# The first batch's last state sums inside the last head group, and its chain ahead of the second batch's behind the loop

## What is computed

```python
x = x + L0_xattn(layernorm(x), ctx, ctx)      # 16 heads, 2048 keys, causal
x = x + L0_attn(layernorm(x), ...)            # state space scan, 16 states
x = x + L0_ffn(layernorm(x), ...)             # router, top 2 of 16 low rank experts
x = x + L1_xattn(layernorm(x), ctx, mask)     # one head, 2048 keys, masked
x = x + L1_attn(layernorm(x), ...)            # 16 heads, local window, compressed blocks, rotary tables
x = x + L1_ffn(layernorm(x), ...)             # top 2 of 8 experts of three layers
```

```python
x_proj = einsum('bld,ed->ble', x, W_xproj)
dt = softplus(x_proj[..., :256]); B = x_proj[..., 256:272]; C = x_proj[..., 272:]
A = -exp(A_log)
h = exp(dt * A) * h + dt * B * x              # per token, 256 channels x 16 states
y = einsum('bdn,bn->bd', h, C) + D * x
```

## Time and profile before

| | us |
|---|---|
| median of 3 runs | 481.57 (479.76 to 482.05) |
| profiled execution | 479.39 |
| its span, on which all times inside the trace are counted | 477.6 |
| PE busy | 417.9 |
| DVE busy | 331.0 |
| ACT busy | 270.2 |
| POOL busy | 103.5 |

### The profile page before, as it was taken

One profiled execution on the slowest core, in us unless ns is written; L12 is line 12 of the kernel. 1 busy time (PEld: TensorE's weight loads), 2 busy tenths in 40 slices (PEclk: granted clock), 3 DMA queues, 4 the chain that ended last, 5 costly groups with the idle time before them and its releaser, 6 DMA issues.

```text
span 477.6 us, 9148 instructions
## 1 busy us (share of the span) xinstructions
PE 417.9 (87%) x3661; PEld 308.8 (65%) x3661; DVE 331.0 (69%) x537; ACT 270.2 (57%) x596; POOL 103.5 (22%) x86
## 2 busy tenths in 40 slices
PE   0178799998979898998999999997999799999997
PEld 0125466666646586567543654347999699999996
DVE  3888775769576975987239843874775587787772
ACT  4404888775848834740233724557950566777752
POOL 3002257001078001000003320440020302333300
PEclk9999999999999999999999999999999989999999
DMA  6599185455553054707500000009400884540000
GB/s 232 128 242 298 20 221 151 124 123 145 149 207 86 1 179 132 289 2 301 228 0 0 2 1 0 0 8 355 168 1 2 279 286 149 183 160 2 1 2 22
DMA packets 25003, 58.28 MB, mean 122 GB/s; under 512 B 5210, under 2 KB 13690, under 8 KB 21115
## 3 DMA queue, kind: packets, MB, share of 16 engines
q1 hardware_dynamic: 24960, 57.69, 37.9%
HBM read 44.77 MB, written 0.29 MB: 94 GB/s over the span
## 4 chain that ended last, share of the span: by engine, by line
PE 71%; DVE 14%; ACT 8%; issue 5%; DMA 2%; SPq 0%; POOL 0%; ACTq 0%; DVEq 0%; POOLq 0%
PE ps L1300 19%; PE ps L1101 10%; PE ps L930 7%; PE ps L917 5%; PE ps L886 4%; DVE mx L1677 3%; PE ps L1009 3%; ACT reg_b L679 3%; PE ps L1256 3%; PE ps L965 2%; PE ps L1098 1%; PE ps L1027 1%; PE ps L1246 1%; PE ps L1245 1%; PE ps L1153 1%
## 5 line engine op out<-in xcount | busy, mean ns | idle before, releaser
L1677 DVE TENSOR_REDUCE mx<-ps 128x1 f32<-128x1024 f32 x64 | 77.0, 1221 | 36.6 <-PE ps L886 25.3
L679 ACT ACTIVATE reg_b<-ps 128x512 f32<-128x512 f32 x128 | 75.2, 598 | 28.2 <-PE ps L917 19.8
L917 PE MATMUL ps<-qreg,reg_b 98*128 98x128 bf16 x512 | 46.9, 225 | 5.2 <-ACT reg_b L679 3.8
L1300 PE MATMUL ps<-part_a 128*128 128x256 f32 x384 | 48.2, 283 | 0.4 <-DVE part_a L1834 0.4
L1101 PE MATMUL ps<-reg_b,xT 128*128 128x512 f32 x96 | 47.6, 618 | 0.0
L917 PEld LDWEIGHTS ps<-qreg,reg_b 98*128 98x128 bf16 x512 | 35.5, 100 | 18.5 <-ACT reg_b L679 8.9
L1300 PEld LDWEIGHTS ps<-part_a 128*128 128x128 f32 x384 | 46.9, 192 | 0.6 <-DVE part_a L1834 0.6
L828 ACT ACTIVATE reg_a<-ps,b 128x256 f32<-128x256 f32 x64 | 30.2, 471 | 26.4 <-PE ps L1300 26.4
L930 PE MATMUL ps<-reg_b 128*32 128x128 f32 x1024 | 43.2, 286 | 0.0
L886 PE MATMUL ps<-reg_b,qreg 96*128 96x512 bf16 x96 | 34.1, 424 | 10.3 <-DMA reg_b<-reg_b 7.5
L1834 DVE TENSOR_TENSOR part_a<-reg_a,part_a 128x256 fp32r<-128x256 f32 x64 | 26.9, 436 | 23.2 <-ACT part_a L831 23.2
(11 more groups left out here) (279 smaller groups left out, 857.0 us busy)
## 6 DMA issues: line engine op xcount, KB each, us to landing
reg_b<-in_w SPq DMA_DIRECT2D x16, 512.0 KB, 8.5
reg_b<-in_w SPq DMA_DIRECT2D x8, 1024.0 KB, 7.8
reg_b<-reg_b SPq DMA_DIRECT2D x56, 128.0 KB, 3.5
reg_b<-in_w_qkv SPq DMA_DIRECT2D x3, 2048.0 KB, 7.4
reg_b<-reg_a SPq DMA_DIRECT2D x40, 128.0 KB, 3.1
reg_a<-in_ctxK SPq DMA_DIRECT2D x4, 1024.0 KB, 7.0
reg_a<-in_ctx SPq DMA_DIRECT2D x8, 512.0 KB, 5.0
reg_b<-bc_mem SPq DMA_DIRECT2D x4, 1024.0 KB, 5.6
```

The source lines that it names most:

```text
L679: sc.activation(pT[n % 3], score_b[n % 2], ACT.Exp).then_inc(S("exp_done"), 1)
L917: mm = pe.matmul(cols, kS[g % 3][0:SROWS, c // 8, j, P * (c % 8):P * (c % 8 + 1)], qT[b][0:SROWS, HPG * hg + j, :], start=not last, stop=True)
L1300: mm = pe.matmul(out, left[u], right[v], start=(i, u, v) == (0, 0, 0), stop=(i, u, v) == (len(terms) - 1, 0, 1))
L1677: ve.reduce_max(mx[:, piece // 2, piece % 2:piece % 2 + 1], score_a[m % 2].rearrange("p i k -> p (i k)"), X_AXIS).then_inc(S("max_done"), 1)
```

## The change

Nothing is computed otherwise. On PE the state sums of half 0 start one pair of chunks earlier (beside chunks 7, 9, 11, 13), half of the sums of half 1 goes beside chunk 15, and the other half between the last values and `outputs_to_rows`. Behind the loop batch 0's norm, transpose and first products go ahead of batch 1's on every engine; `tables()` on DVE moves forward from behind `add_inputs(1)` to the place where `state_input(0)` stood, and `state_input(0)` goes behind `ln_apply(3, 0)`. The fillers get other counts. SP issues eleven loads of `tab_in` ahead of `bias0` and the keys of batch 0, once the last scores of the loop are made; `wkv`, `b_kv` and `b3` are counted on `lora_in`, and their users wait for that.

```diff
+            sp.wait_ge(S("score_b"), NCH * NG)
             load(cos2, io["cos2"], "tab_in")
...
             load(b_c, io["bc"].unsqueeze(0), "tab_in")
 
+            sp.wait_ge(S("hc_done"), KD)
+            load(bias0, io["bias0"].partition_broadcast(P), "ssm_in")
+            load(ctxT[:, 0, :, :], io["ctxT"][0].rearrange("(h p) k -> p h k", p=P), "ctxT_in0")
+
+            sp.wait_ge(S("x_done1"), 1)
+            load(wkv, io["wkv"].rearrange("(k p) n -> p k n", p=P), "lora_in")
...
             spread_maps(1)
...
+            inv_sqrt(2, 0)
             inv_sqrt(1, 1)
-            inv_sqrt(2, 0)
...
+            transposed_x(2, 0)
+            hidden_exp(0)
             transposed_x(1, 1)
-            transposed_x(2, 0)
             copy_z(1)
             softplus_exp(1)
-            hidden_exp(0)
+            gap_exp(0)
             softplus_log(1)
+            wxaT(0)
             exp_table()
...
             for i in range(4):
-                beside[7, 9 + 2 * i] = [(sum_states, 0, 0, range(4 * i, 4 * i + 4))]
+                beside[7, 7 + 2 * i] = [(sum_states, 0, 0, range(4 * i, 4 * i + 4))]
+            beside[7, 15] = [(sum_states, 0, 1, range(NS // 2))]
...
             values(NG - 1, NCH - 1)
+            sum_states(0, 1, range(NS // 2, NS))
             outputs_to_rows(NG - 1)
...
-            sum_states(0, 1)
-            keep_busy(7, 18)
+            keep_busy(7, 20)
+            x_to_columns(2, 0)
+            keep_busy(7, 4)
+            lora_products(0)
             x_to_columns(1, 1)
...
             def tables():
+                ve.wait_ge(S("tab_in"), 176)
...
             add_inputs(0)
+            add_states(0)
+            ln_stats(2, 0)
             weigh_outputs(1)
+            ln_apply(2, 0)
             normalise(1)
...
-            state_input(0)
+            tables()
             lora_add(0)
             ln_stats(3, 0)
             bias_parts()
             ln_apply(3, 0)
+            state_input(0)
             scan(1, 0)
+            max3(0, 0)
             state_input(1)
-            max3(0, 0)
             max3(0, 1)
```

## The result

| | before | after |
|---|---|---|
| median of 6 runs, us | 480.8 (479.69 to 482.05) | 477.03 (475.97 to 478.56) |
| profiled execution, us | 479.39 | 478.56 |
| its span | 477.6 | 476.8 |
| its mean granted clock of TensorE | 0.986 | 0.982 |

The changed kernel takes 0.9926 of the time of the one before, with a 95% interval of 0.9897 to 0.9955: 3.8 us less by the medians. The forecast was 480.5 and 1.1 us of gain, the range 477.7 to 482.4.

A forecast was written before the change was run, and what follows sets the result against it. PE bounds the kernel (71% of the chain), DVE has 14%. Gains of 0.1 and 1.0 us make 1.1: 479.39 becomes 478.3 us profiled, plus 2.2 carried to the median gives 480.5, range 477.7 to 482.4.

The forecast's parts named there:

- The loop's end: At the end of the loop, batch 0's state sums would end at 178.3 instead of 179.6, gaining 1.3 us.
- The third rival: Sums in the loop delay ACT's last exponentials, so the loop doesn't give its 1.3 us: 481.8 us, chance 0.09.
- Batch 0 up to its third norm: Behind the loop, batch 0's third norm would move from 197.75 to about 196.35, 1.4 us gained.
- What is late next: On DVE, the scan waits for ACT's decays, so the second maximum comes at 208.1 against 208.23: gain shrinks to 0.1 us.
- the first rival: DVE doesn't hold the second maximum, as with decays made sooner: 2.5 us gained, 479.1 us, chance 0.12.
- The rest: Up to batch 0's fourth-norm transpose, moving `tables()` removes PE's wait: 1.0 us more, 1.1 us in sum.
- The step that failed: Profiled forecast 478.3 us plus the 2.2 us by which the old profiled execution lay under its median: 480.5 us.
- The wait of 1.11 us goes: PE's wait for DVE's norm ahead of batch 0's transpose at 224.91 would vanish.
- The second rival: TensorE's clock falls behind a 1.3 us stand ahead of `exp3(0)`'s transposes: 0.5 us slower, 482.1 us, chance 0.18.
- the fourth rival: B's read back through memory lands late and holds up the scan by 1.45 us: 481.9 us, chance 0.05.
- The rule on the table load: On ACT, the skill's 1380 ns drain per table switch would cut the gain to 0.6 us; the trace's 1.28 us was taken.

The follow-up runs named there:

- e7: Changed kernel with `tables()` back between `add_inputs(1)` and `add3(0)`: ratio to the old kernel 0.9966, section 67.37 us.
- e2: Changed kernel run and profiled once more, nothing edited: ratio to the old kernel 0.996.
- e3: Changed kernel with the state sums back at their old places in and behind the loop, the new order behind it kept: ratio to the old kernel 0.9991.
- e11: Changed kernel with 18 fillers between the first and second layer of the first expert, in the wait at 378: ratio to the old kernel 0.9928.
- e8: Changed kernel with 13 instead of 8 of the first half's decays ahead of ACT's copy of the third transpose: ratio to the old kernel 0.9933.
- e4: Old kernel with only the state sums moved into the loop, the order behind it as before: ratio to the old kernel 1.0083.
- e6: Old kernel with 16 more fillers ahead of `lora_logits(0)` and 10 ahead of batch 0's fourth transpose: ratio to the old kernel 0.9966.
- e12: Changed kernel with 13 decays ahead of the copy, twelve more fillers ahead of the third transpose and 18 in the expert layer: ratio to the old kernel 0.9881.
- e1: Old kernel run and profiled once more, nothing edited: ratio to itself 1.0008.

## Why the prediction was right or wrong

**The loop's end** held. The sums of half 1 were to start at 173.9 and did at 174.81 - 0.88 = 173.93; they were to end at 178.3 and did at 178.37. The third rival, a loop that doesn't give its 1.3 us, fell with that.

**Batch 0 up to its third norm** held: `add_states(0)` forecast 178.4, measured 178.64; `lora_hidden(0)` 184.65 and 184.67; the third norm 196.35 and 196.49. The loads for the tables made no one wait.

**What is late next** held: scan 200.15 and 200.32, second maximum 208.1 and 208.25 without a wait, p3's transposes behind a wait of 1.3 and 1.34. Eight decays behind the copy decided it, as the first rival's condition said, and five more decays ahead of it gave 1.11 us. That rival was put at 2.5 us in all; with its condition made true the section is shorter by 68.41 - 65.99 = 2.4.

**The rest** held in its sum, 1.1 forecast and 1.31 measured in the section, but not in its reasons. The transpose was to start at 223.8 and did at 224.53 - 0.88 = 223.65. I had taken a length of 3.73 us for the state sums, while the transpose starts 3.57 us behind their start. And I gave the credit to the tables. The runs showed what that move does. In after batch 0 is no earlier at p3's transposes than before (53.65 us behind the first mark, and 211.12 - 157.49 = 53.63 by the row below) and gains at the norm behind them; with the tables back (e7) it is 1.03 earlier at the transposes and gains nothing more. The move takes the lead away in front and gives it back behind. PE before, at these transposes:

```profile
211.12 2.19 PE L1019 MATMUL ps<-cf,reg_b 128*128 128x128 f32 x16
```

**The step that failed** is the last of the sum: "I carry the difference over to the median: 480.5 us." The profiled execution itself was forecast at 478.3 us and took 478.56, in part by luck, since it came 0.88 us late into the section. The step then added 2.2 us, because before's profiled execution lay that far under the median of three runs. After's lay 478.56 - 477.03 = 1.5 us above its median of six. These 2.2 + 1.5 = 3.7 us, less the 0.3 by which the profile was missed, are the whole way from 480.5 to 477.03. Of the 2.2, 0.8 were the small sample: with six runs the median of before is 480.8, not 481.57. The rest of the two offsets goes with the clock. After's profiled execution had a mean granted clock of 0.982, its other five runs 0.986 to 0.993; before's had 0.986, where all its runs have a mean of 0.982. The bound of the range, 477.7, allowed 1.5 us for the median's own moving. The median of after's six runs lies 0.7 us under that bound, and the mean of all 18 runs, 478.3, lies in the range.

**A term that was missing** stands in "The wait of 1.11 us goes", priced at its length alone. I had read that the clock stayed at 1.00 behind it and took this for a property of the place. It was one execution. In 3 of 10 traces the clock fell there, for 1.64 us. The second rival counted a fall of the clock only for the new kernel, with the old one as if it had none; so about half a microsecond, by the estimate above, had no term. The same mistake stands in the fourth rival: the read back of B was priced as a risk of after, and was in the way of before, by 0.52 us in one of six traces. Both together would have moved the forecast by 0.6 us, which is the smaller part of the miss.

**The second rival** fell. PE waits 1.33 to 1.35 us ahead of p3's transposes in five traces (after, e2, e3, e7, e11), and the clock fell behind none of them.

**The rule on the table load.** The load at 192.80 took 1.28 us and the next ACT instruction began 1.29 us after its start, as at the earlier trace rows. No drain shows. The 1380 ns of the Trainium skill, "ScalarE: Activation LUTs", section "What ACT_TABLE_LOAD costs", are not in these traces, and the working by the row was the better one.

**What was on either side of the section** was to stay as it was. It did: from the second mark to batch 1's scores 28.92 us in both profiled executions.

## What to carry to other kernels

Follow the section between two marks that the change doesn't touch, in each trace, and put it beside the medians: here the section repeated within 0.15 us, but for one wait of 0.52 that the trace named, while whole executions moved by over 3 us. When the clock may fall behind a wait of PE, price the wait in the old kernel too, by its length and by the share of executions in which a fall follows, and look at several executions for that share. Don't carry one execution's distance from its median over to another kernel: see first where its granted clock lies among those of the other runs. And when work is put ahead of an engine's copy for the path, count what was moved behind it: five small ACT instructions behind it cost 1.1 us, nearly what the section won.

## What the runs showed of the hardware

- **A wait's length alone doesn't decide whether the clock falls.** Behind 1.11 us (and 0.55 more, a product later) it fell to 1.2 GHz in 3 of 10 traces, behind 1.34 us in none of 5, behind 1.47 us (ahead of the third transpose in after, e2, e3, e8 and e11) in none of 5, behind 1.82 us in 5 of 9, behind 2.1 us in 15 of 16, and in e11, where the filler had made 0.70 of that, once more. The same wait in the same kernel has a fall in some executions and not in others. What PE did ahead of the wait differs between these places: 26 fillers stand ahead of the wait of 1.34, state sums ahead of that of 1.11. Whether that decides was not tested.
- **Falls came in one size.** In all 18 traces a fall is 3.4 us at 0.50, which takes 1.7 us worth of full clock, or two of these in a row; only the one at the end of the span is shorter. Its price hangs on the place: 1.64 us in the projections at 228, 1.4 us at 185 in e4, 0.1 us at 188, where fillers and waits stand behind it.
- **In the last block** a fall is on the path. From the product behind the wait at 378 to the end it is 96.06 us without a fall (e2), 96.8 to 98.3 with one and 98.1 to 98.8 with two.
- **Products that nobody reads can win time.** With nothing but 26 of them more in two waits of before (e6) the ratio was 0.9966 (0.9937 to 0.9995), with the section as it was. With the filler behind `hidden1(0)` and the shorter path of e8 the clock of e12 fell at 141 and once more at 472, at the end of the work, and nowhere else; the mean granted clock of its trace was 0.995, against 0.986 before.
- **The round trip of a small tile through memory is uneven.** The store of 16 KB ahead of B's read back took 2.1 us to land in e1 and 1.4 us in the first trace of before, and the read back can only be issued behind it: 0.7 us, more than the wait of 0.52. The DMA issues of e1:

```profile
bc_mem<-bc_rows SPq DMA_DIRECT2D x1, 16.0 KB, 2.1
```
